# One ring of three PSUM banks for everything TensorE turns, and a third tile copied by ScalarE in some steps of a graph attention kernel

## What is computed

```python
# layer 1, four heads (units 0 to 3), then once more over their concatenation (unit 4, GAT2)
scores = jnp.einsum('...nd,...md->...nm', h, h)
attn = softmax(where(mask, scores, NEG), axis=-1)
out = jnp.einsum('...nm,...md->...nd', attn, h) + b
# layers 2 and 3 (units 5 and 6, ADD1 and ADD2)
e = left[:, :, None] + right[:, None, :]
e = where(e >= 0, e, slope * e)
out = softmax(where(mask, e, NEG), axis=-1) @ h
# each layer: x = layernorm(x + layer(x))
```

## Time and profile before

| | us |
|---|---|
| median of three runs (5706.20 to 5715.72) | 5710.56 |
| the profiled execution | 5713.95 |
| its span, first to last instruction | 5712.2 |
| TensorE busy | 5265.8 (92%) |
| VectorE busy | 4372.0 (77%) |
| ScalarE busy | 3731.8 (65%) |
| GpSimd busy | 1942.3 (34%) |

### The profile page before, as it was taken

One profiled execution on the slowest core, in us unless ns is written; L12 is line 12 of the kernel. 1 busy time (PEld: TensorE's weight loads), 2 busy tenths in 40 slices (PEclk: granted clock), 3 DMA queues, 4 the chain that ended last, 5 costly groups with the idle time before them and its releaser, 6 DMA issues.

```text
span 5712.2 us, 132229 instructions
## 1 busy us (share of the span) xinstructions
PE 5265.8 (92%) x52922; PEld 4508.6 (79%) x52922; DVE 4372.0 (77%) x7325; ACT 3731.8 (65%) x5501; POOL 1942.3 (34%) x1724
## 2 busy tenths in 40 slices
PE   8499999999999899999999999999999999999966
PEld 6388787888878788887878878787888878788755
DVE  5677678778787877778787787878788787877866
ACT  3266557676676757667576666767576675767665
POOL 3400025133341523325241343415233252413466
PEclk9799999999999999999999999999999999999988
DMA  5200000000000000000000000000000000000000
GB/s 177 61 16 11 18 9 9 9 14 14 9 9 11 17 12 7 9 18 12 15 5 10 17 14 9 9 11 16 11 9 9 18 12 15 5 9 18 13 1 5
DMA packets 138241, 95.95 MB, mean 17 GB/s; under 512 B 96032, under 2 KB 115104, under 8 KB 137632
## 3 DMA queue, kind: packets, MB, share of 16 engines
q1 hardware_dynamic: 137632, 87.49, 6.1%
HBM read 35.55 MB, written 8.91 MB: 8 GB/s over the span
## 4 chain that ended last, share of the span: by engine, by line
PE 67%; issue 12%; DVE 6%; POOLq 6%; DVEq 2%; ACT 2%; POOL 1%; DMA 0%; SPq 0%; ACTq 0%
PE po L1067 22%; PE tp L1042 22%; PE pss L1030 9%; PE pss L1031 9%; POOLq L257 6%; DVE pt L1333 3%; DVE rows L1321 2%; PE px L988 2%; DVEq L257 1%; PE px L1055 1%; PE px L1005 1%; ACT rows L1234 1%; PE px L969 1%; PE px L1015 0%; POOL shut L866 0%
## 5 line engine op out<-in xcount | busy, mean ns | idle before, releaser
L1042 PE MATMUL tp<-ident,rows 128*128 128x128 f32 x14336 | 1948.1, 278 | 234.5 <-DVE pt L1333 193.3
L1333 DVE COPY pt<-tp 128x512 f32<-128x512 f32 x2048 | 1332.8, 686 | 921.1 <-PE tp L1042 912.1
L1234 ACT ACTIVATE rows<-rows,nm 128x2048 f32<-128x2048 f32 x896 | 1795.0, 2003 | 323.3 <-DVE nm L1321 321.2
L1042 PEld LDWEIGHTS tp<-ident,rows 128*128 128x128 f32 x14336 | 1600.9, 141 | 476.8 <-issue 308.2
L1067 PE MATMUL po<-pt,hn 128*64 128x128 f32 x28672 | 1782.8, 278 | 37.5 <-ACT ot L1195 36.3
L1067 PEld LDWEIGHTS po<-pt,hn 128*64 128x64 f32 x28672 | 1568.5, 138 | 192.4 <-issue 191.7
L1186 ACT COPY pt<-tp 128x512 f32<-128x512 f32 x1536 | 837.9, 589 | 769.7 <-PE tp L1042 760.9
L869 POOL TENSOR_TENSOR rows<-sr,mask 128x2048 f32<-128x2048 f32 x256 | 1048.7, 4098 | 514.7 <-PE tp L1042 508.4
L1030 PE MATMUL pss<-ha 128*128 128x512 f32 x2560 | 1062.9, 415 | 13.1 <-DMA ha<-hb 12.0
L1031 PE MATMUL pss<-ha,hb 128*128 128x512 f32 x2560 | 1009.5, 394 | 0.0
L1321 DVE CUSTOM_DVE_ANT_0 rows<-pss,mask,nm 128x1024 f32<-128x1024 f32 x640 | 821.7, 1284 | 88.2 <-issue 3.5
(11 more groups left out here) (108 smaller groups left out, 3220.6 us busy)
## 6 DMA issues: line engine op xcount, KB each, us to landing
hb<-ha SPq DMA_DIRECT2D x164, 128.0 KB, 2.3
ha<-hb SPq DMA_DIRECT2D x164, 128.0 KB, 2.3
adjb<-in_adj SPq DMA_DIRECT2D x32, 512.0 KB, 5.6
xin<-x SPq DMA_DIRECT2D x36, 128.0 KB, 2.5
xb<-in_x SPq DMA_DIRECT2D x16, 256.0 KB, 3.0
x<-t SPq DMA_DIRECT2D x16, 256.0 KB, 2.4
xb<-x SPq DMA_DIRECT2D x8, 512.0 KB, 4.0
out<-xb SPq DMA_DIRECT2D x32, 128.0 KB, 1.9
```

What stands on the lines that cost most here:

```text
L1042: last = nc.tensor.transpose(tp[q % 2][:, r * P:(r + 1) * P], rows[:, row.slot, jb * P:(jb + 1) * P], ident[:])
L1234: nc.scalar.activation(rows[:, row.slot, :], rows[:, row.slot, :], ACT.Exp, scale=-1.0, bias=nm[:, row.place, 1:2], accum_out=rs[:, row.pl ...
L1333: nc.vector.tensor_copy(pt[:, CH * q:CH * (q + 1), row.k % SLOTS, :], tp[q % 2][:].rearrange("p (j n) -> p j n", n=P)).then_inc(pt_dve, 1)
```

## The change

The two `tp` banks and `px` become one ring of three. Every use of a bank by TensorE (T0 to T3, B, and each side task with a PSUM result) takes the next bank in program order and waits until the copy of the use three places earlier has been made. ScalarE and VectorE find the bank by the place of the use in the segment. In a step with no side task the uses are T0, T1, B, T2, T3 (even) and T0, T1, T2, T3 (odd).

Tile 2 of a GAT or additive row is copied by ScalarE instead of VectorE where VectorE has a side task in that step and the row of the next step isn't additive, for rows that are not worked on ahead. By the lists of the planner that is 8 rows of the prologue, 25 of each turn of the loop and 9 of the epilogue: 192 copies.

For head rows `take_sums` copies `po` straight to `zt`, without a wait for `ot` to come free, and GpSimd multiplies in place there. The tasks ahead of the prologue become a segment `START` of their own and use the ring too.

```diff
                 for q in range(NC):
                     by_dve = q >= 2 if row.gat else q >= 1
+                    if q == 2 and AHEAD <= k < self.blocks:
+                        by_dve = not (DVE_SIDE & names_at.get(len(self.rows) + 2, set()) and
+                                      gat_at.get(len(self.rows) + 3, True))
...
+        for s in self.steps:
+            turned = self.row(s - 2)
+            uses += self.side_uses(s)
+            uses += [("turn", turned.k, q) for q in (0, 1) if turned]
+            uses += [("back", r.pair) for r in (self.back(s),) if r]
+            uses += self.side_uses(s + 0.5)
+            uses += [("turn", turned.k, q) for q in (2, 3) if turned]
+        self.use = {key: n for n, key in enumerate(uses)}
...
-        tp = [ctx.enter_context(nc.psum_tensor(f"tp{i}", [P, BANK], F32)) for i in range(2)]
+        ring = [ctx.enter_context(nc.psum_tensor(f"ring{i}", [P, BANK], F32)) for i in range(BANKS)]
         po = ctx.enter_context(nc.psum_tensor("po", [P, BANK], F32))
-        px = ctx.enter_context(nc.psum_tensor("px", [P, BANK], F32))
...
-                    nc.gpsimd.tensor_tensor(dst, ot[:], ob[:].rearrange("p r n -> p (r n)"), ALU.mult)
+                    nc.gpsimd.tensor_tensor(dst, dst, ob[:].rearrange("p r n -> p (r n)"), ALU.mult)
...
+            def take(*key):
+
+                n = taken[0]
+                assert where[0][0].use[key] + where[0][1] == n, key
+                taken[0] += 1
+                if freed[n % BANKS]:
+                    pe.wait_ge(*freed[n % BANKS])
+                return ring[n % BANKS]
+
+            def give(count, n):
+
+                freed[(taken[0] - 1) % BANKS] = count.sem, n
...
             def turn(row, q):
 
-                if q >= 2:
-                    wait_copy(row, q - 2)
-                elif row.before:
-                    wait_copy(row.before, q + 2)
+                tile = take("turn", row.k, q)
...
+                count = copied[row.copier[q]]
+                give(count, count.n + row.count[q] + 1)
...
-                px_free()
-                nc.tensor.transpose(px[:, 0:P], turned, ident[:]).then_inc(back_ready, 1)
-                px_used(back_c)
+                tile = take("back", row.pair)
+                nc.tensor.transpose(tile[:, 0:P], turned, ident[:]).then_inc(back_ready, 1)
+                handed(back_c)
...
             def take_sums(row):
 
+                wait(pv_c, pv_c.n + row.pair + 1)
+                if row.unit < H:
+                    nc.scalar.copy(zt[:, row.unit, row.t // 2, :], po[:, 0:P]).then_inc(ot_ready, 1)
+                    return
                 if row.pair or back_c.n:
-                    used = out_c if where[0].behind_head(row) else back_c
-                    wait(used, used.n + row.pair)
-                wait(pv_c, pv_c.n + row.pair + 1)
+                    wait(back_c, back_c.n + row.pair)
```

More of the change, by code:

```diff
@@ L53 @@
 RING = 4
+BANKS = 3
+DVE_SIDE = {"low", "la", "lb", "lc", "ld", "ra", "rb"}
+SIDE = ("xn", "xt", "proj", "hn", "h", "r")
 PROJ = {GAT2: 0, 0: 1, 1: 0, 2: 1, 3: 0}
@@ L84, in __init__ @@
         k = n_gat = n_add = act_tiles = dve_tiles = 0
+        names_at, gat_at = {}, {}
+        for step, name, _, _ in tasks:
+            names_at.setdefault(int(step), set()).add(name)
+        for n, pair in enumerate(r for q in order for r in ([q] * 2 if q else [None])):
+            gat_at[n] = not pair or pair[0] <= GAT2
         if ahead:
@@ L104, in __init__ @@
         blocks = [r for r in self.rows if r]
-        for before, row in zip([None] + blocks, blocks):
-            row.slot_user, row.before = row.k - RING, before
+        for row in blocks:
+            row.slot_user = row.k - RING
         own = [r for r in blocks if r.k < self.blocks]
@@ L115, in __init__, with side_uses @@
             self.tasks.setdefault(step, []).append((name, unit, c))
-        assert all(k == "before" or int(k) in self.steps for k in self.tasks), self.tasks.keys()
+        assert all(int(k) in self.steps for k in self.tasks), self.tasks.keys()
+        uses = []
+        for s in self.steps:
[6 more added lines that the diff above has]
+        self.use = {key: n for n, key in enumerate(uses)}
+        assert len(self.use) == len(uses)
+    def side_uses(self, key):
+        return [task for task in self.tasks.get(key, []) if task[0] in SIDE]
     def tasks_at(self, step):
@@ L126, in odd @@
         return row if row and row.odd else None
-    def behind_head(self, row):
-        earlier = [r for r in self.rows if r and r.k == row.k - 2]
-        return earlier[0].unit < H if earlier else False
     def back(self, step):
@@ L141, in sequence @@
     def sequence(self):
-        return [(s, *task) for s in sorted(k for k in self.tasks if k != "before") for task in self.tasks[s]]
+        return [(s, *task) for s in sorted(self.tasks) for task in self.tasks[s]]
     def tally(self, *names):
@@ L162, in prologue @@
     order = [pair for u, hn in ((0, 1), (1, 2), (2, 1), (3, 2)) for pair in pairs_of(u, hn)] + [None] * GAP
-    tasks = [("before", "xn", 0, c) for c in range(NC)]
-    tasks += [("before", name, 0, g) for g in range(2) for name in ("proj", "low", "hn")]
+    tasks = []
     for u in range(H - 1):
@@ L173, in prologue, with start @@
     return Segment(order, False, True, tasks)
+def start():
+    tasks = [(0, "xn", 0, c) for c in range(NC)]
+    return Segment([], False, False, tasks + [(0, name, 0, g) for g in range(2) for name in ("proj", "low", "hn")])
 def next_head(first):
@@ L233, in epilogue @@
     return Segment(order, True, False, tasks)
-PROLOGUE, LOOP, EPILOGUE = prologue(), main_loop(), epilogue()
+START, PROLOGUE, LOOP, EPILOGUE = start(), prologue(), main_loop(), epilogue()
 class Count:
@@ L247, in run_segments @@
 def run_segments(run):
+    run(START)
     run(PROLOGUE)
@@ L935, in _ @@
             rc_c = Count(rc_ready)
-            px_copied = [None]
+            taken, freed, where = [0], [None] * BANKS, [None]
             def wait(count, n=None):
@@ L944, in wait_copy, with handed @@
                 wait(count, count.n + row.count[q] + 1)
[L946 to L950, removed]
+            def take(*key):
[7 more added lines that the diff above has]
+                freed[(taken[0] - 1) % BANKS] = count.sem, n
+            def handed(count):
                 count.n += 1
-                px_copied[0] = count
+                give(count, count.n)
             def run_task(name, unit, c):
@@ L956, in run_task @@
                 if name == "xn":
-                    px_free()
+                    px = take(name, unit, c)
                     xin_c[c % 2].n += 16
@@ L962, in run_task @@
                     last.then_inc(xn_psum, 1)
-                    px_used(xn_c)
+                    handed(xn_c)
                 elif name == "xt":
-                    px_free()
+                    px = take(name, unit, c)
                     xr_c.n += 1
@@ L970, in run_task @@
                     last.then_inc(xt_psum, 1)
-                    px_used(xt_c)
+                    handed(xt_c)
                 elif name == "proj":
-                    px_free()
+                    px = take(name, unit, c)
                     if unit == GAT2:
@@ L990, in run_task @@
                     last.then_inc(proj_psum, 1)
-                    px_used(hc_c)
+                    handed(hc_c)
                     halves_c.n += 64
                 elif name == "hn":
-                    px_free()
+                    px = take(name, unit, c)
                     wait(hc_c)
@@ L999, in run_task @@
                     last.then_inc(hn_psum, 1)
-                    px_used(hn_c)
+                    handed(hn_c)
                 elif name == "h":
-                    px_free()
+                    px = take(name, unit, c)
                     wait(xt_c)
@@ L1017, in run_task @@
                     last.then_inc(right_psum, 1)
-                    px_used(sr_c)
+                    handed(sr_c)
             def dot_products(row):
@@ L1034, in turn @@
             def turn(row, q):
-                if q >= 2:
-                    wait_copy(row, q - 2)
-                elif row.before:
-                    wait_copy(row.before, q + 2)
+                tile = take("turn", row.k, q)
                 for r in range(CH):
                     jb = CH * q + r
-                    last = nc.tensor.transpose(tp[q % 2][:, r * P:(r + 1) * P],
+                    last = nc.tensor.transpose(tile[:, r * P:(r + 1) * P],
                                                rows[:, row.slot, jb * P:(jb + 1) * P], ident[:])
                 last.then_inc(tr_ready, 1)
+                count = copied[row.copier[q]]
+                give(count, count.n + row.count[q] + 1)
             def turn_back(row):
@@ L1073, in run_segment @@
             def run_segment(segment):
-                for task in segment.tasks.get("before", ()):
-                    run_task(*task)
```

(24 more changed lines are left out.)

1 line of the change is left out of this document (removed).

## The result

The changed kernel takes 5992.1 us (median of four runs, 5987.7 to 5994.3) against 5712.1 for the kernel before beside it: a ratio of 1.049, 95% interval 1.0472 to 1.0508. The direction was forecast, the size was not: 280 us of loss instead of 190, and 7 us above the upper end of the range.

The account below looks back on a forecast made before the run. TensorE's order of work plus its standing still was taken as the bound. 5714 + 151 (loop waits) - 2 (`START`) + 5 (epilogue) + 35 (clock) = 5903, forecast as 5900 us at the median; range 5800 to 5985.

Parts of the forecast that it names:

- What bounds the kernel, and which wait is added: Whole kernel: TensorE, 92% busy, sets the end; T0 of odd additive steps newly waits for `ob`, about 100 waits, 230 to 300 us.
- the wait removed in even steps is worth nothing: Even additive steps: T0 loses its wait for VectorE, but TensorE only arrives earlier and waits longer for `ob`; gain 0.
- The sum for steps 33 to 61: Odd additive steps among GAT rows, each turn: T0 later by 1.1 to 2.6 us each, 17.1 us with step 81.
- The ADD2 stretch: Steps 101 to 111 of each turn: five T0 start before `ob` is done, 9.0 us in all; 6.5 taken.
- The GAT steps 8 to 31: GAT steps behind VectorE side tasks, each turn: T0's wait goes, 2.9 us, of which 2 taken as gain.
- The sum of the waits: Each turn of the loop: 17.1 + 6.5 - 2 = 21.6 us more, 151 us for seven turns.
- the clock: Loop: granted clock falls behind some 14 long stops a turn; 5 us a turn, 35 in all, between 0 and 120.
- The rival with this price, 6036: Loop: waits come and the clock falls after nearly each, 24 us a turn, 6036 us in all; chance 0.12.
- my sum without the clock: Whole kernel: 5714 us plus 151 for the loop's waits, -2 for `START` and +5 for the epilogue; 5868 us.
- The faster rival: Whole kernel: `ob` done before the even step's T3 ends, so T0 never waits; about 5500 us, chance 0.05.

Follow-up runs that it names:

- with the clock held: Changed kernel, with 12 unused 128x128 matmuls into free columns of `po` ahead of T0 of each odd additive step; 5841.3 us, ratio 1.023.

## Why the forecast was right in direction and wrong in size

**What bounds the kernel, and which wait is added.** Right in all but the size of a turn. In the changed kernel 115 turns wait for `ob`, 310 us (forecast: about 100, 230 to 300 us), the wait for VectorE's `pt` fell to 47 us (forecast: below 60), TensorE's busy share fell by 2 points, and T0(37) starts right behind `ob`. A turn of the loop takes 707 us where 690 to 700 were forecast. The wait alone, put into the kernel before, makes the whole loss.

**That the wait removed in even steps is worth nothing.** Right. T0(36) starts sooner, and TensorE then waits 0.61 us for ScalarE's copy of `po` (the line at 2294.70), and later for `ob`.

**The sum for steps 33 to 61.** The forecast was 15.2 us for these eight (17.1 with step 81). With the clock held at 1.00 they cost 13.7 us. In the changed kernel TensorE stands still for 191.59 - 162.39 = 29.2 us of the stretch, and before for 165.18 - 152.94 = 12.2, so 17.0 more. Right: the forecast lies between the two.

**The ADD2 stretch.** 6.5 us were taken. The windows from T0(100) to T0(112), before, after, and with the clock held:

```profile
2597.66:2668.94 71.28, 58.82 (x664) 48.95 (x662) 59.93 (x97) 61.56 (x80) 58.49 (x42) 0.98 0.07 18
```
```profile
2699.82:2781.96 82.14, 64.03 (x663) 55.34 (x662) 57.57 (x98) 63.02 (x81) 59.05 (x42) 0.88 0.06 16
```
```profile
2641.28:2716.15 74.87, 71.08 (x808) 63.90 (x806) 57.92 (x98) 62.22 (x81) 59.34 (x43) 1.00 0.07 18
```

TensorE stands still for 18.1 us instead of 12.5, which is 5.6 more. With the clock held the stretch is 3.6 us longer than before. This is no exact price of the bare wait either: the kernel before, at a clock of 0.98, pays some 1.4 us there (0.02 of 71.3) that this run doesn't, and four of the six odd steps have added matmuls that outlast the stop. So 3 to 6 us came where 6.5 were taken, and the rest of the 9.0 was absorbed; that GpSimd absorbs it was not tested. The GAT steps 8 to 31 gain 151.5 - 148.4 = 3.1 us from T0(8) to T0(32), where 2 were taken.

**The sum of the waits.** 21.6 us for each turn, 151 for seven. TensorE stands still in the loop for 157 us more than before, 22.4 for each turn. Right.

**The step that failed: the clock.** It stood in the sum with 35 us, 5 for each turn, between 0 and 120, as what comes on top of the falls that the kernel before has already. With the same matmuls TensorE is busy in the loop for 120 us longer, 17 for each turn. The run with the clock held says the same in another way: it gives 141 us back in the loop, 20 for each turn, and of these the kernel before pays some 25 itself, which leaves 116, and the own time of the added matmuls hides a little more. The 25 can be read from the run with `ob` between the lifts, which has the same matmuls at a clock of 1.00, where TensorE is busy for 4409.8 us and not 4435.2:

```profile
705.27:5292.48 4587.21, 4409.78 (x45586) 3809.84 (x45585) 3582.86 (x6042) 3277.73 (x4907) 1602.96 (x1428) 1.00 0.05 12
```

So the clock makes some 120 of the 277 us, more than two fifths, where the sum had 35. The term was taken from step 91, where the clock fell behind 2.43 us of idleness in three turns of seven; this share was given to 14 stops and then halved. The stops are longer (3.00 us in step 37), and the fall comes behind most of them: in steps 32 to 61 the clock is 0.93. The upper end of the term, 14 falls of 1.7 us in each turn, would have been 24 us a turn, nearer to the 17 to 20 that came than the 5 that I took; I wrote it down as 120 for the whole where 7 x 24 is 168. The rule of the Trainium skill named there, that short pauses between groups of matmuls make the clock swing, stands on the page "TensorE: Matmul & The Clock Gate" in the section behind the one that I named, "A second HAM failure mode: psum-queue depth-cycling". In the changed kernel it held behind the stops of 3.00 us and more, and not behind those of 2.5 us in step 81 and, in six turns of seven, in step 33. The row from the kernel before was the weaker guide. The rival with this price, 6036, had been given 0.12. The profiled execution with the clock held took 5842 us, where my sum without the clock was 5868. This does not show the rest of the sum to be too high: the held clock also gives back the 25 us that the kernel before pays.

**The faster rival.** It fell for this kernel, and it was the right idea for the next: with `ob` done ahead of T3's end the ring does gain, 99 us by the medians beside it (5617.6 against 5716.8), not the 200 that I gave it. TensorE still waits 102 us for VectorE's copies, and 91 us for `po`:

```profile
PE ring L1073 <- DVE pt L1379: 101.6, 89, 3.5
PE po L1100 <- ACT zt L1231: 65.3, 71, 1.7
...
PE po L1100 <- ACT ot L1235: 26.0, 16, 2.6
```

## What to carry to other kernels

When several kinds of results share one ring of banks, a take can wait for the copy of another kind of result than its own, made by another engine. Go through the uses in program order, and for each one find the copy of the use as many places back as there are banks and what stands ahead of that copy on its engine. A short result whose copy stands behind a long instruction must not be followed by a take that lands on its bank: move that copy forward into a gap, or the take of the bank backward in the order. And where TensorE will stop for some microseconds again and again, price the matmuls behind each stop at the low clock as well, unless the trace shows them at the high one behind stops as long.

## What the runs showed of the hardware

Granted clock and duration in step 37: behind a stop of 3.00 us T0 and T1 took 1.94 us instead of 1.09 to 1.16, and the window behind it has a granted clock of 0.77, a mix of the two levels of 1.2 and 2.4 GHz:

```profile
2300.77:2307.70 6.93, 6.90 (x55) 6.12 (x56) 2.65 (x6) 3.32 (x5) 1.03 (x2) 0.77 0.01 2
```

Two stops of the same turn of the changed kernel, of 2.51 us in step 33 and of 3.00 in step 41, and the 7 us behind each:

```profile
2277.62 0.63 PE L1073 MATMUL ring<-ident,rows 128*128 128x128 f32 x4 [2.51 <-ACT ob L1242]
```
```profile
2277.62:2284.62 7.00, 7.00 (x70) 6.10 (x72) 4.24 (x7) 3.81 (x6) 1.00 (x2) 1.00 0.01 2
2325.44:2332.44 7.00, 7.00 (x51) 6.25 (x51) 1.16 (x4) 3.43 (x5) 1.00 (x2) 0.59 0.00 0
```

Behind the first the clock stayed at 1.00, and behind the second it was 0.59 in that stretch. The length of the stop alone doesn't decide it: with the wait alone, without the ring, the 2.52 us of step 33 were followed by a clock of 0.76 over 7 us in all seven turns. The stop of 1.03 us in the run with `ob` ahead of the exponential left T0 and T1 at 1.06 us and its stretch at a clock of 1.00. And the 24 matmul instructions that fill a stop for nothing, 2.84 us in step 37, made the kernel 151 us faster: the matmuls behind the stop ran at the high clock. I had not expected a gain of 2.5% from work thrown away.
